# Sums over keys moved back into the visit, their copy one step earlier, and the layernorm's small operations of GpSimd and VectorE put at other steps

## What is computed

```python
q = (queries @ Wq.T + bq).reshape(B, Nq, HEADS, D_K).transpose(0, 2, 1, 3)   # B=8, Nq=224, D_K=32
k = (keys @ Wk.T + bk).reshape(B, Nk, HEADS, D_K).transpose(0, 2, 1, 3)      # Nk=750
v = (values @ Wv.T + bv).reshape(B, Nk, HEADS, D_K).transpose(0, 2, 1, 3)
att = jax.nn.softmax(jnp.einsum('bhqd,bhkd->bhqk', q, k) / np.sqrt(D_K), axis=-1)
out = jnp.einsum('bhqk,bhkd->bhqd', att, v).transpose(0, 2, 1, 3).reshape(B, Nq, 512)
out = queries + out @ Wo.T + bo
out = (out - mean) / jnp.sqrt(var + 1e-05) * gamma + beta
```

## Time and profile before

| | us |
|---|---|
| median of 3 runs (lowest to highest) | 647.19 (646.28 to 649.47) |
| time of the profiled execution | 648.4 |
| its span, first to last instruction | 646.5 |
| TensorE matmul busy in the span | 621.7 (96%) |
| VectorE busy | 474.8 (73%) |
| GpSimd busy | 458.8 (71%) |
| ScalarE busy | 351.9 (54%) |

### The profile page before, as it was taken

One profiled execution on the slowest core, in us unless ns is written; L12 is line 12 of the kernel. 1 busy time (PEld: TensorE's weight loads), 2 busy tenths in 40 slices (PEclk: granted clock), 3 DMA queues, 4 the chain that ended last, 5 costly groups with the idle time before them and its releaser, 6 DMA issues.

```text
span 646.5 us, 14824 instructions
## 1 busy us (share of the span) xinstructions
PE 621.7 (96%) x5217; PEld 424.2 (66%) x5217; DVE 474.8 (73%) x680; ACT 351.9 (54%) x673; POOL 458.8 (71%) x443
## 2 busy tenths in 40 slices
PE   9989999999999998999999999999999999998994
PEld 7756676766666665666766667666677666764542
DVE  4677677777777586776788677876887768766895
ACT  5424556556565564654655655654565636544661
POOL 9301686875978588585889849775887858777852
PEclk9999999999999998999999999999999999997998
DMA  9367633562256623745037632476237521331020
GB/s 307 115 177 163 145 91 74 128 142 69 64 124 140 127 55 84 155 96 148 25 84 167 143 77 62 100 142 143 54 87 167 98 61 32 88 92 35 2 59 28
DMA packets 96021, 67.09 MB, mean 104 GB/s; under 512 B 69892, under 2 KB 82192, under 8 KB 95952
## 3 DMA queue, kind: packets, MB, share of 16 engines
q1 hardware_dynamic: 95952, 66.16, 42.9%
HBM read 24.52 MB, written 3.67 MB: 44 GB/s over the span
## 4 chain that ended last, share of the span: by engine, by line
PE 81%; DVE 9%; POOL 4%; ACT 2%; issue 2%; POOLq 0%; ACTq 0%; DVEq 0%
PE ps_task L594 37%; PE ps_scores L605 12%; PE ps_task L645 9%; PE ps_scoresT L629 9%; PE ps_task L553 6%; DVE top L911 3%; POOL pair_sums L1019 2%; PE ps_task L671 2%; PE ps_scores L594 2%; DVE attn_sums L918 1%; POOL head_sums L1027 1%; DVE attn_parts L933 1%; ACT probsT L792 1%; POOL head_sums L1024 1%; PE ps_scores L573 1%
## 5 line engine op out<-in xcount | busy, mean ns | idle before, releaser
L792 ACT ACTIVATE probsT<-ps_scoresT 125x448 f32<-125x448 f32 x384 | 204.0, 545 | 198.5 <-PE ps_scoresT L629 183.5
L911 DVE TENSOR_REDUCE top<-ps_scores 112x1 f32<-112x750 f32 x256 | 236.1, 929 | 90.7 <-PE ps_scores L605 89.4
L1019 POOL TENSOR_TENSOR pair_sums<-probsT 125x672 f32<-125x672 f32 x122 | 200.2, 1641 | 116.4 <-ACT probsT L792 107.6
L629 PE MATMUL ps_scoresT<-stacks 100*125 100x224 f16 x768 | 135.5, 261 | 0.9 <-ACT probsT L792 0.4
L594 PE MATMUL ps_task<-wvT,ctxT 128*125 128x512 f16 x564 | 135.3, 379 | 0.9 <-DVE parts L868 0.9
L605 PE MATMUL ps_scores<-stacks 96*112 96x512 f16 (+1 forms) x512 | 127.2, 331 | 6.0 <-DVE top L911 3.7
L594 PE MATMUL ps_task<-ctxT,wkT 128*128 128x375 f16 x708 | 131.9, 325 | 0.1
L629 PEld LDWEIGHTS ps_scoresT<-stacks 100*125 100x125 f16 x768 | 94.1, 137 | 40.3 <-ACT probsT L792 5.5
L1027 POOL TENSOR_TENSOR head_sums<-head_sums,pair_sums 125x224 f32<-125x224 f32 x122 | 90.5, 742 | 9.6
L1024 POOL TENSOR_TENSOR head_sums<-pair_sums 125x224 f32<-125x224 f32 x122 | 89.1, 730 | 10.4
L594 PEld LDWEIGHTS ps_task<-wvT,ctxT 128*125 128x125 f16 x564 | 73.3, 136 | 33.3 <-DVE parts L868 1.1
(11 more groups left out here) (100 smaller groups left out, 520.9 us busy)
## 6 DMA issues: line engine op xcount, KB each, us to landing
stacks<-parts SPq DMA_DIRECT2D x256, 60.9 KB, 2.0
ctx_in<-in_ctx SPq DMA_DIRECT2D x8, 768.0 KB, 5.5
stacks<-parts SPq DMA_DIRECT2D x128, 46.9 KB, 2.0
resid<-in_x SPq DMA_DIRECT2D x8, 448.0 KB, 3.9
ctx_in<-in_ctx SPq DMA_DIRECT2D x7, 512.0 KB
out_y<-y SPq DMA_DIRECT2D x16, 224.0 KB, 2.3
x_in<-in_x SPq DMA_DIRECT2D x8, 256.0 KB, 3.1
stacks<-parts SPq DMA_DIRECT2D x128, 14.0 KB, 1.8
```

The source lines that it names most:

```text
L629: last = nc.tensor.matmul(ps_scoresT[0:KP, piece % 2, NQ * i:NQ * i + NQ], stacks[:, g, h, KP * k:KP * k + KP], stacks[:, g, h, Qc], start ...
L792: nc.scalar.activation(probsT[0:KP, g % 2, h, 2 * j:2 * j + 2, :].rearrange("p k q -> p (k q)"), ps_scoresT[0:KP, piece % 2, 0:2 * NQ], AC ...
L911: nc.vector.tensor_reduce(top[0:QP, g % 2, HG * q + h:HG * q + h + 1], ps_scores[0:QP, s % RING, 0:NK], AX.X, ALU.max).then_inc(top_ready, 1)
L1019: nc.gpsimd.tensor_tensor(pair_sums[0:KP], probsT[0:KP, g % 2, h, 0:3, :], probsT[0:KP, g % 2, h, 3:6, :], ALU.add).then_inc(pair_sums_rea ...
```

## The change

`sum_keys` goes from the end of step 2 to step 1, right behind the attend, and the copy on ScalarE from step 3 to step 2. On GpSimd both `rstd_of` go to step 25, behind the head sum of step 24, and `plus_beta` to steps 26 and 28. On VectorE the second `times_gamma` goes from step 29 to step 28, the first stays in 26. The first `plus_beta` keeps its place between the head sums of steps 24 and 28; the second moves from behind the head sum of step 29 to ahead of it, behind that of step 28. `SPREAD` and `TAIL` are untouched.

```diff
-    SUMS_BEHIND = 2
-    STAGES = {**{("attend", k): (2, VISIT) for k in range(KT)}, "sum_keys": (2, SUMS_BEHIND), "copy": (2, 3), ("invert", 0): (2, 4),
+    STAGES = {**{("attend", k): (2, VISIT) for k in range(KT)}, "sum_keys": (2, VISIT), "copy": (2, 2), ("invert", 0): (2, 4),
...
-    GAMMA_STEPS = (3 * UNIT + 2, 3 * UNIT + 5)
+    RSTD_STEP = 3 * UNIT + 1
+    GAMMA_STEPS = (3 * UNIT + 2, 3 * UNIT + 4)
...
-                    if s % UNIT != SUMS_BEHIND:
-                        for u, g_u in due("sum_keys", b, s):
-                            sum_keys(u, g_u)
+                    for u, g_u in due("sum_keys", b, s):
+                        sum_keys(u, g_u)
...
-                    if s % UNIT == SUMS_BEHIND:
-                        for u, g_u in due("sum_keys", b, s):
-                            sum_keys(u, g_u)
...
-                            if s == O_STEPS[q] + 2:
+                            if s == RSTD_STEP:
                                 rstd_of(q, b - 1)
-                        for q in range(2):
-                            if s == GAMMA_STEPS[q] + 1 and not (isinstance(b, int) and b == B):
+                            if s == GAMMA_STEPS[q] and not (isinstance(b, int) and b == B):
                                 plus_beta(q, b - 1)
```

## The result

The changed kernel takes 663.38 us (median of 6 runs, 661.97 to 664.87) against 647.96 for the kernel before (6 runs, 646.28 to 649.47) on the same chip: ratio 1.0242, 95% interval 1.0222 to 1.0261. The profiled execution is the 663.38, its span 661.5, 15.0 more than before. I had forecast 652.4 with 660 as the upper end: the direction was right, the loss three times as large.

The account below looks back on a forecast made before the run. TensorE, busy 139.06 of 140 us, was taken as the bound. Against the profiled 648.4: -7.7 + 2.2 + 2.3 + 8.4 = +5.2, giving 652.4 us for the median; own range 649 to 656, 8 in 10 within 643.5 to 660.

Parts of the forecast that it names:

- rival A: The six long new waits on TensorE also lower its clock, at 1.2 us each: +7, 659.5 us; chance 0.20.
- the first visits: Step 1 of iterations 2 and 4 to 7: TensorE waits 1.2 to 2.1 us for GpSimd's fourth head sum, 8.4 in all.
- 3.33 each, 10.0: GpSimd's three heads after the second beta, before a first visit: 3.33 us each, 10.0 in all, ending at 412.2.
- Merging saves 0.28 a visit, 0.03 given back: Sums appended to the attend save 0.28 us in 28 visits, 7.8; a later piece is 0.03 short in 21, 0.6.
- The 0.2 that I took back at each first visit: Step 2 of a batch's first unit: ScalarE's cast leaves the piece's exponential 0.2 us short, 7 visits, 1.4 us.
- The fourth visits 0.55 late: Step 25, iterations 1 to 4: TensorE waits 0.55 us each for GpSimd, 2.2 in all; iterations 5 and 6 0.
- The fourth visit of iteration 0 at 2.3: Step 25 of iteration 0, no layernorm yet, GpSimd two heads behind: TensorE waits 2.3 us for the head sum.
- Edits priced at nothing: Earlier copy, stores and second gamma ahead of step 29's V copy cost 0; at most 1 us an iteration for gamma.
- B: GpSimd is in time, without the rstd waits and gamma collision: 639.5 to 644 us, faster; chance 0.12.
- C: Fourth visits in time, first visits 0.9 us late: gains and waits sum to 0, about 647 us; chance 0.23.
- D: The sums block in step 1 costs as much as in step 2, the 7.8 not saved: 658 us; chance 0.03.

Follow-up runs that it names:

- experiment 1: The kernel before with only the sums and the copy moved, all layernorm work where it was: 665.84 us, ratio 1.0260.
- experiment 2: The changed kernel with sums and copy back where they were, so only the layernorm moves remain: 645.03 us, ratio 0.9958 to the kernel before.
- experiment 8: The changed kernel with sums and copy moved only at steps 9 and 17, left in steps 2 and 3 of the other visits: 641.32 us, ratio 0.9906.
- experiment 3: The changed kernel with the second beta on GpSimd behind head 1 again, its gamma still in step 28: 652.76 us, ratio 1.0067.
- experiment 5: The changed kernel with the second gamma in step 27 instead of 28, its beta still ahead of head 1: 663.18 us, ratio 1.0233.
- experiment 4: The changed kernel with the attend run twice in the six visits where TensorE waits over 1.5 us: 656.51 us, ratio 1.0131.
- experiment 9: The changed kernel with the low part of the attention result written by a single-input VectorE operation, without the subtraction: 662.63 us, ratio 1.0213.
- experiment 10: The changed kernel with sums and copy of one visit, step 25 of iteration 0, left in steps 2 and 3: 658.57 us, ratio 1.0161.
- experiment 6: The changed kernel with the second beta on VectorE right behind its gamma, instead of on GpSimd: 655.65 us, ratio 1.0133.

## Why the prediction was wrong, step by step

The kind of wait, its places and the direction were right. Two steps failed. The larger one: the sum priced a wait at its own length and left the clock behind it to rival A, where it cost 7.5 us. The other: the first visits were 8.4 in the sum and were 12.8, mainly because GpSimd's three heads took longer than "3.33 each, 10.0".

**Merging saves 0.28 a visit, 0.03 given back: right.** The undisturbed visits took 0.20 to 0.27 less. In the steps themselves: step 17, with the visit, takes 0.38 more, which is the two rounds, and steps 18 and 19 take 0.65 less. The 0.2 that I took back at each first visit did not come: iteration 1's, which waits for nobody, gained 0.22.

**The fourth visits 0.55 late: right.** Measured waits 0.61, 0.61, 0.61, 0.60, and the old 0.5 gone. In iterations 5 and 6 I said 0; they waited 0.5, and gained 0.44 even so, because VectorE no longer held the attend there.

**The fourth visit of iteration 0 at 2.3: right in its wait** (2.48), but the steps cost 4.08, with the clock.

**The first visits: the term that was too small.** I had beta's end at 402.2; it was at 409.51, which is 402.13 on the old scale. The step that failed is the next: "3.33 each, 10.0". The three heads took 11.22 (409.51 to 420.73). I had taken their price from two heads that lost only 0.33 to VectorE. The first of the three began 2.5 us later against TensorE's list than before. The next long add then ran beside VectorE's low part (L929) and lost 1.03, and two adds of the last head lost 0.32 each beside VectorE's split of the inputs (L884, 417.29, 2.92 for two). Before, only one of those two had lost 0.33, and the collision with the low part had been VectorE's loss, 1.11 for an operation of 0.43. I had also the differences between iterations wrong: 2.43, 2.43, 2.49, 2.56 and 1.89, not 2.1, 2.1, 1.5, 1.5, 1.2. That these waits come from the sums' move is shown by experiments 1, 2 and 8; that 0.9 of each comes from beta's place, by 3. Its division is shown in part by 3 and 5 together: with gamma earlier the waits lose 0.5 and the long add still takes 2.63 to 2.65; with beta behind head 1 no long add ahead of the first visits takes over 1.88, and the waits lose 0.4 more.

**The clock: rival A, which I had at 0.20, is what happened,** though its own sum, 659.5, was 3.9 short. I priced a fall at up to 1.6 and six of them at 1.2; five came at 1.5 (experiments 4 and 5). With the real waits, the forecast's own sum: gains -7.7 and 1.4 of the take-back that didn't come; first visits 12.8 (the five waits and 0.2 each for the attend's last round) in place of 8.4; falls 7.5; less 2.0 in iteration 3. There the hold at the loop's turn was followed by a fall before and not after, and this 2.0 is luck: in experiments 1, 2, 3, 5, 9 and 10 the clock did fall there. -9.1 + 2.2 + 2.7 + 12.8 + 7.5 - 2.0 = 14.1 of 15.0.

**The clock is partly chance.** In the profiled executions of the changed kernel and the experiments it never fell in the middle of the launch behind a wait of 1.91 us or less, and behind those of 1.94 to 2.56 it fell in 20 of 26. It fell behind one of three waits of 1.94 and not behind one of 2.48 in experiment 5; one of 2.31 in experiment 1, one of 2.31 in experiment 9 and one of 2.44 in experiment 10 passed without. So the length of a wait alone doesn't decide it; what else does is open. The turn of the loop and the last units (before: one and two falls) change from kernel to kernel by 1.6 to 3 us, with and without a fall in the same way, which is more than some of the effects compared here.

**Edits priced at nothing: right.** In experiment 2 the maxima don't hold TensorE in steps 29 to 31 of iterations 1 to 6, and merged visits with the copy in step 2 gained what the sums' rounds explain. **Rivals B, C and D:** B and C needed GpSimd earlier than it was; D is refuted by the undisturbed visits.

## What to carry to other kernels

Moving a consumer two steps earlier is free only where its slowest input has that much slack; read it at every kind of visit, and do it only there (experiment 8: same edit, half the places, and the sign of the result turns). When an in-order engine is filled, an instruction that must wait for a partner goes behind the work others wait for, not ahead of it. And price a hold of TensorE of about 2 us or more with the clock that may fall behind it: here 2.5 us of wait mostly cost 4.

## What the runs showed of the hardware that was not expected

- A hold of 1.58 us cost 1.57 and one of 2.49 cost 3.9, while one of 2.44 with no fall behind it cost 2.42 (experiment 10): the stretch at the lower level adds 1.5 as a step, not in proportion.
- GpSimd and VectorE lose to each other by turns for the same pair of operations: the low part took 1.11 instead of 0.43 before the change, and after it 0.43 while GpSimd's add took 2.64 instead of 1.61; the scaling (L919) took 0.38 before and 1.80 after. In the records it isn't the later one that loses: the add had begun at 412.72, the low part began at 413.46 and kept its 0.43. The Trainium skill, SBUF — State Buffer, Who interferes with whom, which I drew on in the prediction, has the one that comes second wait; L919 beside the add begun 0.06 before it agrees, this pair does not, as far as starts on GpSimd can be read. Nor does the same L919 begun 0.14 behind an add in the last units (it keeps 0.37, the add takes 1.98). A single-input VectorE form (experiment 9) didn't spare GpSimd. In the last units of the changed kernel:

```profile
601.92 1.98 POOL L1015 TENSOR_TENSOR pair_sums<-probsT 125x672 f32<-125x672 f32 x1
...
602.06 0.37 DVE L919 TENSOR_TENSOR attn_sums<-attn_sums 128x224 f32<-128x224 f32 x1
```

- Beta, 0.69 on VectorE at the end of the launch, took 1.98 in the middle beside GpSimd (experiment 6), more than GpSimd's own 1.27.
